# Second layer's experts over gathered blocks of rows instead of whole chunks, with its fronts moved into the attention

## The reference

```python
xn = _layernorm(x)                       # first layer
x = x + attention(xn) + experts64(xn)    # 16 heads of 8; 64 experts, 3 a row, 64 rows each at most
xn = _layernorm(x)                       # second layer
x = x + rwkv(xn) + experts8(xn)

def rwkv(x):                             # a recurrence along the 1024 rows of a batch
    r, v, k = split(x @ W_rvk.T)
    out = (sigmoid(r) * wkv_scan(-exp(time_decay), time_first, k, v)) @ W_out.T

def experts8(xm):                        # 8 experts, 128 -> 256 -> 128, 2 for each row
    probs = softmax(xm @ Wg)
    topk_p, topk_i = top_k(probs, 2)
    for e in range(8):
        ye = relu(xs @ W1[e] + b1[e]) @ W2[e] + b2[e]
        y = y + (e_sorted == e)[:, None] * ye
    out = zeros.at[tok_idx].add(y * p_sorted)
```

## Time and profile before

| | |
|---|---|
| three runs | median 526.85 us (525.44 to 527.23) |
| profiled execution, its span | 525.1 us (the page gives no other time for it) |
| PE busy | 494.3 us, 94% |
| ACT busy | 375.1 us, 71% |
| DVE busy | 303.1 us, 58% |
| POOL busy | 144.1 us, 27% |

### The profile page before, as it was taken

The page is one execution under the profiler, slowest core; times in us unless marked ns, Lnnn a source line. Parts: engine busy times, 40 slices in busy tenths (PEclk is TensorE's granted clock), DMA queues, the critical chain, the costliest instruction groups (busy, mean ns, idle before and its releaser), DMA issues.

```text
span 525.1 us, 11527 instructions
## 1 busy us (share of the span) xinstructions
PE 494.3 (94%) x4696; PEld 270.8 (52%) x4696; DVE 303.1 (58%) x790; ACT 375.1 (71%) x464; POOL 144.1 (27%) x133
## 2 busy tenths in 40 slices
PE   6977999999999999999998999999899999999996
PEld 5874223443455455445444232333467766767775
DVE  6799899434343343343330126367937983994895
ACT  3967988786978878978888989888535625553641
POOL 4078000303203203203000445425550755400120
PEclk8997999999999999999998999999899999999999
DMA  5200000565487877977362511100100110000000
GB/s 148 82 1 1 2 1 2 157 216 181 163 238 243 282 243 218 313 238 233 126 201 60 152 32 31 32 1 21 37 6 0 35 38 11 22 0 1 21 1 20
DMA packets 38542, 50.01 MB, mean 95 GB/s; under 512 B 3581, under 2 KB 20250, under 8 KB 38490
## 3 DMA queue, kind: packets, MB, share of 16 engines
q1 hardware_dynamic: 35524, 43.84, 25.4%
q0 software_dynamic: 2560, 5.25, 5.1%
q10 hardware_dynamic: 406, 0.20, 0.1%
HBM read 45.07 MB, written 4.19 MB: 94 GB/s over the span
## 4 chain that ended last, share of the span: by engine, by line
PE 50%; ACT 17%; DVE 6%; issue 5%; DVEq 0%
ACT region_b L564 11%; PE bank L1361 11%; PE scores L1609 9%; PE bank L1618 9%; PE scores L1347 5%; PE bank L1407 4%; PE bank L1395 3%; ACT xn L570 2%; PE bank L1417 2%; PE bank L1478 2%; DVE region_a L1067 2%; ACT L564 2%; ACT L570 2%; DVE base L1078 1%; PE bank L1372 1%
## 5 line engine op out<-in xcount | busy, mean ns | idle before, releaser
L564 ACT ACTIVATE region_b<-scores 128x1024 f32<-128x1024 f32 x256 | 242.4, 1045 | 51.8 <-PE scores L1347 51.6
L1361 PE MATMUL bank<-region_b 128*16 128x256 f32 x2048 | 149.0, 391 | 0.0
L1347 PE MATMUL scores<-region_b 32*128 32x512 f16 x512 | 83.0, 389 | 14.2 <-ACT region_b L564 14.0
L626 ACT ACTIVATE region_b<-scores,small_cols 128x512 f32<-128x512 f32 x64 | 43.6, 685 | 50.3 <-PE scores L1609 50.3
L388 POOL DMA_INDIRECT region_a<-xn_rows,slot_token x32 | 32.5, 1016 | 160.8 <-DVE h_rows L908 108.0
L1361 PEld LDWEIGHTS bank<-region_b 128*16 128x16 f32 x2048 | 42.0, 96 | 57.9 <-issue 42.6
L1618 PEld LDWEIGHTS bank<-region_a,region_b 128*128 128x128 f32 x512 | 62.2, 192 | 15.5 <-issue 15.3
L1347 PEld LDWEIGHTS scores<-region_b 32*128 32x128 f16 x512 | 20.8, 91 | 92.4 <-ACT region_b L564 68.9
L1618 PE MATMUL bank<-region_a,region_b 128*128 128x128 f32 x512 | 62.5, 275 | 0.0
L1609 PE MATMUL scores<-x_rows,region_a 128*128 128x512 f32 x128 | 62.3, 610 | 0.0
L1078 DVE SCALAR_TENSOR_TENSOR base<-bank,g,base 128x128 f32<-128x128 f32 x128 | 36.0, 344 | 28.0 <-PE bank L1618 27.6
(11 more groups left out here) (243 smaller groups left out, 590.6 us busy)
## 6 DMA issues: line engine op xcount, KB each, us to landing
region_a<-in_L_ffn_w SPq DMA_DIRECT2D x64, 512.0 KB, 5.3
region_a<-in_L_ffn_b SPq DMA_DIRECT2D x17, 128.0 KB, 7.2
slot_out<-slots_io SPq DMA_DIRECT2D x8, 256.0 KB, 7.7
region_a<-in_L_attn_x SPq DMA_DIRECT2D x4, 256.0 KB, 4.5
xn_rows<-xn SPq DMA_DIRECT2D x1, 1024.0 KB, 5.1
region_a<-in_L_ffn_W SPq DMA_DIRECT2D x1, 1024.0 KB, 5.9
out<-base SPq DMA_DIRECT2D x4, 256.0 KB, 2.3
region_a<-xn_rows,slot_token POOLq DMA_INDIRECT x32, 3.7
```

The lines of the kernel that those rows point to most:

```text
L564: a.activation(PR[:, n % PBUF, 2 * h:2 * h + 2, :], S[:, 2 * h:2 * h + 2, :], ACT.Exp, scale=SCALE).then_inc(s["exp_done"], 1)
L626: a.activation(HS[:, e % 2, k], ps[2 * (e % 2) + k][:], ACT.Relu, bias=COL[:, HC1 * e + k:HC1 * e + k + 1]).then_inc(s["relu_done"], 1)
L1347: last = mm(S[:, j], KT[head, hg, keys], QT[head, hg, BLK * c:BLK * c + BLK], start=True, stop=True)
L1361: last = mm(AV[32 * j:32 * j + VW, cols], VA[:, tile, HG * (g % NHG) + j, :], PR[:, st % PBUF, j, cols], start=(st == 0 and half == 0), st ...
```

## The change

For chunks 0 to 2 (1536 rows, `ST_TILES` = 12 tiles, two experts a row, 3072 pairs) each expert's rows are brought together in blocks of 128, each expert's last block filled up: at most 31 blocks (`BLOCKS`), always all 31 run, in 8 groups of four (`GROUPS`). The steps:

- The fronts of chunks 0 to 2 run in the attention, tiles 86 to 123; all time mixes come behind it. `attention_cols(3)` and the rest of chunk 3's front stand between the first groups.
- At tiles 124 to 127 PE counts rows per expert (`counts2`), DVE gives each pair a slot (`slots2`, `block_tables`), PE turns this into row lists (`invert2`), and DVE casts them (`block_tokens`, semaphore `idx2_ready`).
- SP writes both weight matrices to one DRAM tensor `w_both`, and the normed rows to `xn2_rows`. For each block it reads the expert's number into a register and loads that expert's 256 KB; buffers hold two groups.
- POOL gathers 128 rows a block (`blocks_in`), ring of 16 blocks. PE transposes (`turn_blocks`), `block_up`, ACT `block_relus` (a piece for each block, as shifts differ), PE `block_down`, ACT `block_rows`, SP stores to `y2_out`.
- When all groups are stored, POOL gathers the two results of each row (`rows_back`, 24 gathers), and DVE adds them with their weights (`rows_combined`).
- Chunk 3 stays dense, eight steps behind the groups. `slot(u)`, u = 0 to 23, places mixes: two slots a group, then one a dense step; `MIX_AT` gives each chunk's first.
- In the mix two differences (`D2`, `F1`) go from POOL to DVE. The square root of the norm is computed on DVE for all chunks. Gathers of the first layer wait by four lanes instead of by tile.

```diff
-    MIX_FROM = {1: 1, 2: 11, 3: 21}
+    BLOCKS = TOP2 * ST_TILES + E1 - 1
+    MIX_AT = {0: 3, 1: 7, 2: 12, 3: 16}
...
 # SP
+            sp.wait_ge(s["table_ready"], 1)
+            def load_block(g, i, b):
+                e = sp.value_load(EBU[0:1, b:b + 1], min_val=0, max_val=E1 - 1)
+                sp.dma_start(WR[CH * (g % 2) + i], w_both[bass.ds(e, 1)].rearrange("e p n -> p (e n)")).then_inc(wr_in[g % 2], 16)
+            for g in range(GROUPS):
+                if g >= 2:
+                    sp.wait_ge(s["s_down"], g - 1)
+                for i, b in enumerate(group_blocks(g)):
+                    load_block(g, i, b)
+                if g >= 2:
+                    store_rows(g - 2)
+            store_rows(GROUPS - 2)
+            store_rows(GROUPS - 1)
+            for c in (0, 1, 3, 2):
+                if c < SPARSE:
+                    sp.wait_ge(s["rows_done"], CH // 2 * (c + 1))
+                else:
+                    sp.wait_ge(s["acc_done"], E1)
...
 # POOL
             def mix(c):
-                g.tensor_tensor(D2, KX, PP[:, 1:BLK + 1], ALU.subtract).then_inc(s["pool_wkv"], 1)
-                g.tensor_tensor(F1, PP[:, 0:BLK], PM, ALU.subtract).then_inc(s["pool_wkv"], 1)
                 pool.wait_ge(s["d_exp"], 4 * c + 2)
                 pool.wait_ge(s["vx_sb"], c + 1)
                 g.tensor_tensor(EV, D2, VX, ALU.mult).then_inc(s["pool_wkv"], 1)
                 pool.wait_ge(s["d_exp"], 4 * c + 4)
                 g.tensor_tensor(T1, F2, VX, ALU.mult).then_inc(s["pool_wkv"], 1)
...
+            pool.wait_ge(s["idx2_ready"], 1)
+            for G in range(5):
+                blocks_in(G)
             mix(0)
+            for G in range(5, GROUPS):
+                blocks_in(G)
             mix(1)
+            for i in range(2):
+                pool.wait_ge(y2_in[i], 16 * GROUPS // 2)
+            for t in range(4):
+                rows_back(t)
             mix(2)
+            for t in range(4, 9):
+                rows_back(t)
             mix(3)
+            for t in range(9, ST_TILES):
+                rows_back(t)
...
 # ACT, behind the attention
+            def slot(u):
+                for y, m in MIX_AT.items():
+                    if u == m - 1 and y:
+                        keys(y)
+                    if u == m + 1:
+                        state_exps(y)
+                        values_in(y)
+                        receptance(y)
+                    if u == m + 2:
+                        output_exps(y)
...
+            for g in range(GROUPS):
+                if g + 1 < GROUPS:
+                    block_cols(g + 1)
+                block_rows(g)
+                slot(2 * g)
+                if g + 1 < GROUPS:
+                    block_relus(g + 1)
+                else:
+                    relus(0)
+                slot(2 * g + 1)
...
 # DVE, behind the attention
+            def slot(u):
+                if u == 0:
+                    x1_norm(NC - 1)
+                if u == 5:
+                    gates_in(NC - 1)
+                if u == 6:
+                    gates(NC - 1)
+                for y, m in MIX_AT.items():
+                    if u == m:
+                        time_mix(y)
+                        time_mix_first(y)
+                    if u == m + 1:
+                        time_mix_states(y)
+                    if u == m + 2:
+                        time_mix_out(y)
+                    if u == m + 3:
+                        time_mix_end(y)
+                    if u == m + 5:
+                        mixed(y)
...
+            for u in range(2 * GROUPS):
+                slot(u)
+            for e in range(E1):
+                accumulate(e)
+                slot(2 * GROUPS + e)
+                if e in (2, 4, 6, 7):
+                    rows_combined((2, 4, 6, 7).index(e))
+            rows_combined(4)
+            rows_combined(5)
...
 # PE
+                if n == 124:
+                    counts2()
+                if n == 127:
+                    invert2()
             for half in range(2):
                 values(TILES - 1, half)
...
+            def slot(u):
+                for y, m in MIX_AT.items():
+                    if y and u == m - 1:
+                        keys(y)
+                    if u == (m + 1 if y else 1):
+                        values_in(y)
+                    if u == (m + 1 if y else 3):
+                        receptance(y)
+                    if u == m + 4:
+                        finish(y)
...
             tokens_out(NG)
+            keys(0)
+            turn_blocks(0)
+            attention_cols(NC - 1)
+            block_up(0)
+            attention_out(NC - 1)
+            for g in range(GROUPS):
+                if g + 1 < GROUPS:
+                    turn_blocks(g + 1)
+                block_down(g)
+                slot(2 * g)
+                if g + 1 < GROUPS:
+                    block_up(g + 1)
+                else:
+                    up2(0)
+                slot(2 * g + 1)
...
```

More of the change, by code:

```diff
@@ new lines, in block_relus @@
+            def block_relus(g):
+                act.wait_ge(s["table_ready"], 2)
+                if g >= 2:
+                    act.wait_ge(s["s_down"], g - 1)
+                for k in range(HC1):
+                    act.wait_ge(s["su_ps"], HC1 * g + k + 1)
+                    for i, b in enumerate(group_blocks(g)):
+                        cols = slice(P * i, P * i + P)
+                        last = a.activation(HS[:, g % 2, k, cols], ps[2 * (g % 2) + k][:, cols], ACT.Relu, bias=B1C[:, b, k:k + 1])
+                    last.then_inc(s["s_relu"], 1)
@@ new lines, in block_rows, with relus @@
+            def block_rows(g):
+                act.wait_ge(s["s_down"], g + 1)
+                if g >= 2:
+                    act.wait_ge(y2_in[g % 2], 16 * (g // 2))
+                n = len(group_blocks(g))
+                a.activation(YB[:, g % 2, 0:n, :].rearrange("p i d -> p (i d)"), ps[7][:, 0:P * n], ACT.Copy).then_inc(s["sy_sb"], 1)
+            def relus(e):
+                for k in range(HC1):
+                    n = HC1 * e + k
+                    act.wait_ge(s["up2"], n + 1)
+                    if k == 0:
+                        if e >= 2:
+                            act.wait_ge(s["down2"], e - 1)
+                        else:
+                            act.wait_ge(s["s_down"], GROUPS - 1 + e)
@@ new lines, in gates @@
+                iota = iota_e[:, 0:E1].unsqueeze(1).to_broadcast([P, CH, E1])
+                for k in range(TOP2):
+                    last = v.tensor_tensor(EQ2[:, k, tiles, :], iota, IXF[:, tiles, k:k + 1].to_broadcast([P, CH, E1]), ALU.is_equal)
+                link(last)
+                if c < SPARSE:
+                    link(v.tensor_tensor(M2[:, tiles, :], EQ2[:, 0, tiles, :], EQ2[:, 1, tiles, :], ALU.add))
+                    for t in range(CH * c, CH * c + CH):
+                        last = v.tensor_tensor(MP2[:, t + 1, :], MP2[:, t, :], M2[:, t, :], ALU.add)
+                        if t < ST_TILES - 1:
+                            link(last)
+                    if c == SPARSE - 1:
+                        last.then_inc(s["mask2_ready"], 1)
@@ new lines, in block_down @@
+            def block_down(g):
+                pe.wait_ge(s["s_relu"], HC1 * (g + 1))
+                if g:
+                    pe.wait_ge(s["sy_sb"], g)
+                else:
+                    pe.wait_ge(s["ep_used"], NG)
+                for i in range(len(group_blocks(g))):
+                    cols = slice(P * i, P * i + P)
+                    for k in range(HC1):
+                        last = mm(ps[7][:, cols], HS[:, g % 2, k, cols], WR[CH * (g % 2) + i][:, H1 + P * k:H1 + P * k + P],
+                                  start=(k == 0), stop=(k == HC1 - 1))
+                last.then_inc(s["s_down"], 1)
@@ L1653 @@
+            for e in range(E1):
+                if e + 1 < E1:
+                    up2(e + 1)
+                down2(e)
+                slot(2 * GROUPS + e)
 _INS = ["L0_attn_x", "L0_attn_ln_w", "L0_attn_ln_b", "L0_attn_qkv_w", "L0_attn_qkv_b", "L0_attn_out_w", "L0_attn_out_b",
```

610 lines of the change are left out of this document (360 added, 250 removed).

## The result

The changed kernel takes 558.81 us (median of four runs, 556.26 to 560.68) against 526.14 for the kernel before beside it: a ratio of 1.063, 95% interval 1.058 to 1.069. So it is slower, as forecast, and inside the range, but by 33 us where 9 were forecast. Without two of the mixes there was a single run. The profiled execution took 556.26 us, with a span of 554.5; my layout had 529.1, and 534.1 with its allowance for the clock. 20.4 us of span have to be accounted for.

A forecast was written before the change was run, and what follows sets the result against it. PE's program order was taken to set the end, ACT and PE binding the attention's last third. Span 525.1, attention +3, groups 77.5 and close 67.6 replacing 144, gave 529.1; plus 5 clock and 1.75: 536 us, range 508 to 560.

The forecast's parts named there:

- my layout: New order summed from the attention on: 76.9 us for groups, 68.2 for the close, span 529.1; 529 to 545 had chance 0.48.
- The mechanism: Behind the attention: PE idle before the first two finish steps, DVE idle some 14 us at chunk 2's scan, released by POOL.
- The rival with PE as the bound: Groups: mixes ready as PE comes by, last block at 443, span 510.5, so 512 us; faster, chance 0.30.
- its upper bound: Whole kernel: the range's upper end, 560 us, for register reads at 2.5 us or most of the cold clock.
- The term of the clock: PE behind the attention: slower work after waits costs some 5 us, bounds 0 and 36.
- four waits: PE's waits of over 2 us with PE next on the path, at 393, 431, 451 and 511 us.
- the wait counted at 393: PE's wait at 393 us, where group 0 reaches PE at 392.6; one of four waits charged some 5 us together.
- the bound of 36 us: Clock's upper bound: all of PE's work on this path, about 36 us, at half rate.
- The term of the attention: Attention up to the block indices: the move costs 3 us, 381 to 384, bounds -2 to +8.
- Logits then at 363: Chunk 2's logits in the attention ready at 363 us, the second exponential of tile 122 some 2 us earlier than 364.5.
- gates of 3.8 us: Chunk 2's gates on DVE in the attention: 2.8 us before, about 3.8 with some six more small operations, ending at 370.5.
- four gathers with their landing: POOL's gathers for group 0: four at 1.31 us and 2.7 to land, reaching PE at 392.6.

The follow-up runs named there:

- the filled run: Changed kernel, PE turning the unused identity matrix before groups' rows and 58, 44, 160 and 20 times before the four finish steps (also called filled whole): 542.86 us.
- The three pieces: Changed kernel with chunk 3's combine on DVE behind the last division, chunk 2's copy ahead of chunk 1's gates, block indices ahead of tables: 552.54 us, ratio 1.050.
- both runs on it: Changed kernel without the register read before each weight load, 556.68 us; changed kernel with 16 weight buffers, loading four groups ahead, 556.49 us.
- three runs on the attention: Changed kernel with chunk 3's combine on DVE, 555.44 us; with that combine waiting for chunk 2's norm, 559.58; with two steps reordered on DVE, 555.59.
- the run of the two swaps: Changed kernel with chunk 2's copy ahead of chunk 1's gates and block indices ahead of the tables in DVE's order: 555.59 us.
- second new order: the new order's first version with chunk 3's combine on DVE, ACT's copy of mix values earlier, POOL's gathers and the tables' second half reordered: 512.38 us, ratio 0.976.
- filled in part: Changed kernel, PE turning the unused identity matrix before groups' rows and 36, 28, 110 and 20 times before the four finish steps: 553.85 us.
- new order and filling: second new order, plus PE turning the identity matrix 14, 12 and 4 times at waits for the inversion, last evacuation and chunk 3's rows: 512.34 us.
- the new order's first version: Changed kernel's work behind the attention reordered engine by engine, mixes earlier, finish steps later, weights four groups ahead, plus two DVE reorderings in the attention: 525.8 us.

## Why the prediction was right in direction and wrong in size

**The mechanism stood.** PE waits at both early finish steps (6.80 and 5.24 us), DVE idles 14.63 us at chunk 2's scan where some 14 were forecast, and POOL's product behind the gathers ends it. Leaving mixes out took 21.7 us from the groups, and changing POOL's order 10.1 from the close, the stages where the layout has these waits. The rival with PE as the bound would have needed mix 0 done by the time PE came; PE stood 6.80 us, and the first finish step began 47.4 us behind the indices, where the layout has 46.8. That the time lies inside the range is no merit of its upper bound, which stood for register reads of 2.5 us (they took 0.47) or for a clock cold most of the time.

**Where the 20.4 us went.** Attention: the indices exist at 392.7 instead of 384, 8.7 (5.0 to 11.7 in the eight executions with this attention). Groups: 84.3 instead of 76.9, 7.4. Close: 77.5 instead of 68.2, 9.3. Less the 5 allowed for the clock, 20.4.

**The term of the clock was mis-sized.** I counted four waits (the third finish step is not among them) and charged one slow step to each, 5 us in all; a slow step was the up product of 3.51 us where another took 1.88, 1.6 more, at a granted clock of 0.50. No run shows those 5 us. The trace after shows half rate over a finish step and one to three steps more: 4.15 us instead of 2.31 for the finish, then 3.31 instead of 1.95 for a down product, or 3.72 instead of 1.88 for an up product. With the waits filled, what lies behind the four finish steps is shorter by 2.4, 4.1, 3.6 and 3.1 us, and the wait counted at 393 gives nothing. The groups then take 78.2 us, against 76.9 in the layout, and the close 70.9 against 68.2. So the clock cost at least 12.7 us of span, not 5. The step that failed was the count of slow steps, taken from one dip in a kernel where PE is otherwise 96% busy; the bound of 36 us erred the other way. That the waits bring the slow steps is in the filled run: behind 0.76 us left of the 6.80 us wait, the first half of the finish took 1.16 us where 2.08 stood.

**The term of the attention was mis-sized.** The sum has 3 us for it, with bounds of -2 and +8; it took 11.7, from 381 to 392.7. The step that failed is "Logits then at 363": they were ready at 374.4, while the steps behind them took 18.3 us instead of 21 (`slots2` 8.5, forecast 8.7). It rested on the fronts' durations of chunk 0, beside which POOL only gathered, and left out that chunk 1's gates stand ahead of chunk 2's copy on DVE. The tables, which stand ahead of the indices, were in the sum with 3.8 us and took 3.9. The three pieces together gave 7.7 us back. I had reckoned with slower DVE instructions beside POOL (1.68 and 1.86 us for 0.75) in the mixes only. Two small sums do not come out either: gates of 3.8 us do not lead from 363 to 370.5, and four gathers with their landing end at 391.9, not 392.6.

**The loads were over-priced.** The register read was 0.47 us, not 1.0, and four loads landed in 3.4 us as against 3: together 7.0 us a group, not 9. This error lay beside the mixes: both runs on it moved the median by about 2 us, within the intervals.

**What is left.** 1.3 us between the groups and 2.7 in the close stay without a run of their own, and so does the scatter of the attention from execution to execution; in the close, even the filled run's steps behind the last finish show half rate (3.34 us for an up product; granted clock 0.50 from 526 to 528 us).

## What to carry to other kernels

When a change takes work off the bounding engine, lay out the queue of every other engine that used to hide beside it: here 24 us less of busy PE made the kernel 33 us slower, and nearly the same work in another order (one combine moved from POOL to DVE, twice the weight buffers) 13 us faster than the kernel before. Price a wait of PE by all the steps that run behind it, not by one: here filling the waits took 2.4 to 4.1 us off what lies behind each finish step, against the 1.6 of one slow step. Where a single fix gains nothing, look in the same trace for what now stands in its place before giving the cause up: here three runs on the attention gave nothing clear of the scatter, and their pieces together 7.7 us.

## What the runs showed of the hardware

Beside POOL's combine (one product of 2.75 us and three additions of 4.00 together) DVE instructions of 0.17 us took 1.1 and more in the kernel after, one-input ones on four numbers among them (L1105 1.44, L1107 1.13), and DVE's combine of 3.49 us took 9.11 in the run of the two swaps. Ahead of a finish step, leftover waits of 2.62 us (second new order) and of 2.67, 3.15 and 6.34 (filled in part) were followed by half rate from that step on (2.07 to 2.08 us for each half of the finish, at a granted clock of 0.50, where 1.15 and 1.16 stood at 1.00). Behind 1.27 us (new order and filling) and 1.62 (filled whole) the finish step ran at full rate (1.16 us for its first half) and the up product after it at half (3.64 us instead of 1.95, 3.34 instead of 1.88); behind 1.62 us in the run filled in part, and behind 0.47 to 0.89 in the one filled whole, neither was slow. In the new order's first version the down product shortly behind a wait of 2.03 us took 3.54 us instead of 1.95, yet an up product behind 2.16 us in the changed kernel took 2.02. In the kernel before, behind a wait of 1.05 us the finish step took 1.16 us for its first half and the up product that came next 3.51 instead of 1.88, so the length of the wait alone does not tell it.
